# A four-layer residual block on one core: a constant matrix multiplied into unused banks by TensorE while it waits, and a deviation taken by logarithm and exponential

## The reference, cut to what matters

```python
x = x + L0(gn(x))   # 1x1 conv, norm, silu; a gate of 6 gaussian bases per group; 1x1 conv, norm, silu
x = x + L1(gn(x))   # the block below
x = x + L2(gn(x))   # 8-head attention over 256 tokens
x = x + L3(gn(x))   # deformable 3x3 convolution (offsets and mask from a 3x3 convolution)
```

```python
mu = jnp.mean(y, axis=-1, keepdims=True)
var = jnp.mean(jnp.square(y - mu), axis=-1, keepdims=True)
y = (y - mu) * jax.lax.rsqrt(var + 1e-05) * ln_g + ln_b
out = jnp.einsum('bld,od->blo', y, W_out)
```

## Time and profile before

| | us |
|---|---|
| median of 3 runs | 549.79 |
| lowest, highest | 548.02, 550.30 |
| the profiled execution: its time | 542.76 |
| the profiled execution: its span | 541.0 |
| mean granted share of TensorE's clock in it | 0.881 |

### The profile page before, as it was taken

The page is one execution under the profiler, slowest core; times in us unless marked ns, Lnnn a source line. Parts: engine busy times, 40 slices in busy tenths (PEclk is TensorE's granted clock), DMA queues, the critical chain, the costliest instruction groups (busy, mean ns, idle before and its releaser), DMA issues. The chain is left out here.

```text
span 541.0 us, 9049 instructions
## 1 busy us (share of the span) xinstructions
PE 408.6 (76%) x3218; PEld 207.1 (38%) x3218; DVE 355.1 (66%) x670; ACT 289.2 (53%) x509; POOL 119.2 (22%) x138
## 2 busy tenths in 40 slices
PE   1325681499999736488999999938269999999995
PEld 1114561245555413323333333325125544455442
DVE  4547786313365696988999998150446878788784
ACT  1459974113223413417888888812737668486441
POOL 4500003100000001864431111010004618156000
PEclk9856986599999985958999999977759999999998
DMA  5300000720000000882210000008674290742302
GB/s 138 116 0 1 0 0 0 146 48 1 0 1 0 1 0 1 233 274 81 80 41 3 4 2 2 2 22 180 155 158 105 52 213 2 175 89 63 70 2 78
DMA packets 21496, 34.35 MB, mean 64 GB/s; under 512 B 5376, under 2 KB 16336, under 8 KB 20688
## 3 DMA queue, kind: packets, MB, share of 16 engines
q1 hardware_dynamic: 17488, 24.94, 19.5%
q10 hardware_dynamic: 2688, 4.16, 3.2%
q0 software_dynamic: 1280, 4.72, 3.0%
HBM read 16.80 MB, written 4.64 MB: 40 GB/s over the span
## 5 line engine op out<-in xcount | busy, mean ns | idle before, releaser
L1259 DVE TENSOR_TENSOR L_s<-L_row_ps,L_cols 128x1024 f32<-128x1024 f32 x72 | 87.7, 1219 | 8.3 <-PE L_row_ps L1390 6.7
L877 DVE TENSOR_REDUCE L_mx<-L_ring 128x2 f32<-128x512 f32 x128 | 83.3, 687 | 10.4 <-PE L_ring L1000 9.9
L932 ACT ACTIVATE L_e<-L_ring 128x512 f32<-128x512 f32 x128 | 73.6, 597 | 20.9 <-PE L_ring L1013 18.9
L1411 PE MATMUL L_acc<-L_s,L_t_sb 128*64 128x256 f32 x576 | 79.8, 399 | 1.1 <-DVE L_s L1259 1.0
L1320 ACT ACTIVATE L_cols<-L_col_ps 128x512 f32<-128x512 f32 x72 | 42.8, 596 | 44.7 <-PE L_col_ps L1398 44.2
L1000 PE MATMUL L_ring<-stacks_k_st,stacks_q_st 64*128 64x256 bf16 x256 | 50.7, 300 | 7.0 <-DVE L_v_all L866 5.5
L1411 PEld LDWEIGHTS L_acc<-L_s,L_t_sb 128*64 128x64 f32 x576 | 35.5, 138 | 35.1 <-DVE L_s L1259 21.2
L1013 PE MATMUL L_ring<-stacks_q_st,stacks_k_st 64*128 64x256 bf16 x256 | 47.0, 281 | 1.7 <-DMA stacks_q_st<-L_m_parts 1.7
L1390 PE MATMUL L_row_ps<-L_hats,L_sel 48*128 48x512 bf16 x144 | 44.5, 391 | 0.0
L1033 PE MATMUL L_ctx_ps<-L_e,L_v_x 128*32 128x256 f32 x512 | 40.7, 391 | 0.0
L1381 PE MATMUL L_acc<-all_w_all,L_xn 64*128 64x192 f32 x96 | 26.3, 356 | 13.9 <-DVE L_t_sb L1239 13.9
(11 more groups left out here) (254 smaller groups left out, 765.4 us busy)
## 6 DMA issues: line engine op xcount, KB each, us to landing
L_hats<-L_parts SPq DMA_DIRECT2D x32, 216.0 KB, 5.0
L_hat<-L_offsets SPq DMA_DIRECT2D x24, 192.0 KB, 4.5
L_mask<-L_offsets SPq DMA_DIRECT2D x12, 192.0 KB, 4.6
stacks_q_st<-L_q_parts SPq DMA_DIRECT2D x12, 128.0 KB, 3.7
stacks_k_st<-L_k_parts ACTq DMA_DIRECT2D x12, 128.0 KB, 5.1
stacks_q_st<-L_q_parts POOLq DMA_DIRECT2D x12, 128.0 KB, 2.7
stacks_k_st<-L_k_parts POOLq DMA_DIRECT2D x12, 128.0 KB, 3.0
L_stack<-L_xpad SPq DMA_DIRECT2D x8, 162.0 KB, 5.7
```

The lines of the kernel that those rows point to most:

```text
L877: dve.tensor_reduce(mx[:, n % 2, :, head], ring[:, place(step) % 3].rearrange("p (q s) -> p q s", q=2), AX.X, ALU.max).then_inc(max_read, 1)
L932: act.activation(e[:, k], ring[:, 3 + v % 3], ACT.Exp, scale=HD2 ** -0.5).then_inc(e_ready, 1)
L1259: dve.tensor_tensor(s[:, q], row_ps[:, q], cols[:, t % 3:t % 3 + 1].broadcast_to([P, 2, 2 * N]), ALU.mult).then_inc(s_ready, 1)
L1411: mm = pe.matmul(acc[C * e:C * e + C, b, 0:N], t_sb[:, b, h, (KK * e + t) * C:(KK * e + t + 1) * C], s[:, q, h, e * N:(e + 1) * N], start= ...
```

## The change

1. **`keep_clock`**, new: `count` matmuls of `avg2` with itself (128x128, float32) into columns 0 to 127 of a PSUM bank that nothing reads at that time. It waits for nothing and signals nothing. It stands on PE at these places, 237 matmuls in all, in order: layer 0: 12 before the first norm and 5 after it, 4 after w_pre's matmuls, 22 after the second norm, 3 after the pooled vector's first matmul, 26 after the third norm (the block's last work on PE). Layer 1: 17 after the norm and ahead of the wait for `g_ready`, 4 ahead of the quads' first, in the last quad 5, 3 and 9 where the other quads have pieces of the next convolution, 14 at the end. Layer 2: 6 after the norm, 5 between the halves of v, 18 ahead of the wait for `v_all_ready`, and 1 in each of the 19 steps with v < 0. Layer 3: 25 after the norm and ahead of the first wait for `stack`, 40 between `weigh(0, 0, ...)` and `weigh(0, 1, ...)`.
2. **Layer 1's deviation**: in place of ACT's root, DVE's reciprocal and DVE's product stand a load of the table set that has logarithm and exponential, ACT's `Ln` of var into a new buffer `lnvar`, ACT's `Exp` with scale -0.5 (this gives 1/sqrt(var)), and DVE's product. In the last quad only `Exp` waits for `added`, not the read of `var`.
3. The layers' own step semaphores become one that the group norms already have. It moves and adds no instruction.

The diff, cut to its core:

```diff
+def keep_clock(pe, avg2, out, count):
+
+
+
+    for _ in range(count):
+        pe.matmul(out[:, 0:P], avg2[:], avg2[:], start=True, stop=True)
+
...
             def _(pe):
                 pe.wait_ge(avg_in, 16)
+                keep_clock(pe, avg2, y1[:, 6], 12)
                 gn_x.tensor(pe)
+                keep_clock(pe, avg2, y1[:, 6], 5)
                 weights.wait(pe, 0)
                 for h in range(NP // 2):
                     pe.wait_ge(xn_ready, 2 * h + 2)
                     pe.matmul(y1[:, 2 * h:2 * h + 2, :], w_pre[:], xn[:, 2 * h:2 * h + 2, :], start=True, stop=True).then_inc(y1_ready, 1)
+                keep_clock(pe, avg2, y2[:, 6], 4)
                 gn_1.tensor(pe)
+                keep_clock(pe, avg2, y2[:, 6], 22)
                 pe.wait_ge(z_ready, NP)
                 pe.matmul(s1, w_s1[:], pooled[:], start=True, stop=True).then_inc(s1_ready, 1)
+                keep_clock(pe, avg2, y2[:, 6], 3)
                 pe.wait_ge(h1_ready, 1)
                 pe.matmul(s2, w_s2[0:32, :], h1[:], start=True, stop=True).then_inc(s2_ready, 1)
                 pe.wait_ge(h2_w_ready, 1)
@@ -369,6 +383,7 @@
                             mm = pe.matmul(y2[:, ds(k, 1), :], w_post[:], t[:, q, j:j + 1, :], start=False, stop=(j == NB - 1))
                         mm.then_inc(t_used, 1)
                 gn_2.tensor(pe)
+                keep_clock(pe, avg2, y1[:, 6], 26)
 
-        o, var, sd = m.sb("o", [P, 2, N]), m.sb("var", [P, 2, N]), m.sb("sd", [P, 2, N])
+        o, var, lnvar, sd = (m.sb(n, [P, 2, N]) for n in ("o", "var", "lnvar", "sd"))
...
                 def over_deviation(q):
 
                     dve.wait_ge(sd_ready, q + 1)
-                    dve.reciprocal(sd[:], sd[:]).then_inc(scaled, 1)
-                    dve.wait_ge(scaled, 2 * q + 1)
                     dve.tensor_tensor(sd[:], o[:], sd[:], ALU.mult).then_inc(scaled, 1)
-                    dve.wait_ge(scaled, 2 * q + 2)
+                    dve.wait_ge(scaled, q + 1)
...
-                def deviation(q):
+                def deviation(q, last=False):
+
+
+                    act.preload_act_table_set("natural_log_exp_and_others")
                     act.wait_ge(o_copied, 2 * q + 4)
-                    act.activation(sd[:], var[:], ACT.Sqrt).then_inc(sd_ready, 1)
+                    act.activation(lnvar[:], var[:], ACT.Ln).then_inc(ln_ready, 1)
+                    act.wait_ge(ln_ready, q + 1)
+                    if last:
+                        act.wait_ge(added, NQ - 1)
+                    act.activation(sd[:], lnvar[:], ACT.Exp, scale=-0.5).then_inc(sd_ready, 1)
...
                 quad(0, True)
                 with act.Fori(1, NQ) as q:
                     quad(q, False)
-                act.wait_ge(added, NQ - 1)
-                deviation(NQ - 1)
+                deviation(NQ - 1, last=True)
 
             @block.tensor
             def _(pe):
                 gn.tensor(pe)
                 weights.wait(pe, 1)
+                keep_clock(pe, avg2, xs_ps[:, 0], 17)
                 pe.wait_ge(g_ready, 1)
...
                         conv_xs(q + 1, 0, 2)
+                    else:
+                        keep_clock(pe, avg2, xs_ps[:, 0], 5)
...
+                keep_clock(pe, avg2, xs_ps[:, 0], 4)
                 for g in range(NQ):
...
+                keep_clock(pe, avg2, xs_ps[:, 0], 14)
...
                 weights.wait(pe, 2)
+                keep_clock(pe, avg2, ring[:, 5], 6)
...
                     pe.matmul(k_bank(g), w_k[:], xn[:, 2 * g:2 * g + 2, :], start=True, stop=True).then_inc(k_ps_ready, 1)
                 for h in range(2):
+                    if h:
...
+                keep_clock(pe, avg2, ring[:, 4], 18)
                 pe.wait_ge(v_all_ready, 2)
...
                     if v + LAG < 8 * B:
                         largest(v + LAG)
+                    if v < 0:
+                        keep_clock(pe, avg2, ring[:, 4], 1)
...
                 weights.wait(pe, 3)
+                keep_clock(pe, avg2, row_ps[:, 1, 1], 25)
                 for g in range(NQ):
                     pe.wait_ge(stack_in[g], 64)
...
                 for k in range(6):
+                    if k == 1:
+                        keep_clock(pe, avg2, acc[:, 1], 40)
                     weigh(0, k, k, k)
```

More of the change, by code:

```diff
@@ L227, in layer0 @@
         avg_in, *x_in = m.sems("avg_in x_in0 x_in1")
-        (own, xn_ready, y1_ready, norm1_ready, z_ready, s1_ready, h1_ready, s2_ready, h2_ready, h2_w_ready,
+        (xn_ready, y1_ready, norm1_ready, z_ready, s1_ready, h1_ready, s2_ready, h2_ready, h2_w_ready,
          par_ready, exp_in, exp_out, coef_ready) = m.sems(
-            "own xn_ready y1_ready norm1_ready z_ready s1_ready h1_ready s2_ready h2_ready h2_w_ready "
+            "xn_ready y1_ready norm1_ready z_ready s1_ready h1_ready s2_ready h2_ready h2_w_ready "
             "par_ready exp_in exp_out coef_ready")
@@ L279, in _ @@
                 dve.sem_inc(norm1_ready, 1)
-                step = Steps(dve, own)
+                step = Steps(dve, signals.own, signals.own_steps)
                 dve.wait_ge(h2_ready, 1)
@@ L316, in _ @@
                 step(dve.tensor_tensor(zc0[:], zc0[:], c0[:], ALU.add))
+                signals.own_steps = step.n
                 with dve.Fori(0, NP // 2) as i:
@@ L476, in layer1 @@
             "conv_ready acts_ready bt_ready xt_ready bt_copied v_ready kv_ps kv_ready y_ps y_own y_ready cen_y sq_ready o_ready var_ready o_copied")
-        added, scaled, sd_ready = m.sems("added scaled sd_ready")
+        added, scaled, sd_ready, ln_ready = m.sems("added scaled sd_ready ln_ready")
         with nc.Block() as block:
@@ L677, in quad @@
                         conv_xs(q + 1, 2, 4)
+                    else:
+                        keep_clock(pe, avg2, xs_ps[:, 0], 3)
                     pe.wait_ge(kv_ready, q + 1)
@@ L683, in quad @@
                         conv_xs(q + 1, 4, 8)
+                    else:
+                        keep_clock(pe, avg2, xs_ps[:, 0], 9)
                     pe.wait_ge(y_ready, 2 * q + 4)
@@ L763, in layer2 @@
         scratch = [nc.dram_tensor(f"L2_{n}_parts", (NQ, 3, 2, HD2, 4, 2, 2 * N), BF16, kind="Internal").ap() for n in "qk"]
[L765 to L766 removed]
+        (xn_ready, q_ps_ready, k_ps_ready, full_ready, hi_ready, mid_ready, parts_ready, v_ps_ready, v_all_ready,
+         pool_own) = m.sems("xn_ready q_ps_ready k_ps_ready full_ready hi_ready mid_ready parts_ready v_ps_ready v_all_ready pool_own")
         stored = m.sems(" ".join(f"stored_{s}{g}" for g in range(NQ) for s in "qk"))
```

7 lines of the change are left out of this document (3 added, 4 removed).

## The result

| | before | changed |
|---|---|---|
| median of 20 runs, us | 548.15 | 551.16 |
| lowest, highest, us | 543.16, 552.69 | 546.99, 556.96 |
| ratio to before, 95% interval | | 1.0069 [1.0039, 1.0100] |
| the profiled execution: span, us | 541.0 | 550.6 |
| mean granted clock in it | 0.881 | 0.911 |

The account below looks back on a forecast made before the run. The prediction saw a low PE clock in the layers' openings and layer 1's reciprocals on the path; terms summed to 11.75, rounded to 12, off the median 549.79 gave 537.8 us, range 532.5 to 545.0.

Parts of the forecast that it names:

- layer 2's part: Layer 2's opening and lead-in: 1.4 us saved in all, with the singles fitting PE's spare time while DVE sets the steps.
- The price: Every added matmul: 0.23 us from the moment the clock is full, 0.43 before.
- rival A: Layer 2's opening and layer 3's weighings: the clock falls again in gaps, gain only 8.5, time 541.3 us; chance 0.28.
- rival C: All blocks: added matmuls do not lift the clock and stay at 0.43 to 0.48; 10 slower, 560 us; chance 0.05.
- Deviation, 3.65: Layer 1's tail: without reciprocals, with logarithm and exponential, 3.65 us saved, or 2.85 if the table load drains.
- Layer 1's opening, 2.2: Layer 1's norm and first quad run faster at the full clock: 2.2 us saved after 0.2 for the barrier.
- The barrier: Before layer 1: the 26 take 8 us and end level with the barrier, at worst 0.35 late.
- Layer 0, 1.8: Layer 0's opening and middle: norm, w_pre's matmuls and those after ACT's silu come sooner, 1.8 us saved.
- Layer 2's opening, 1.4: Layer 2's norm and first matmuls run faster: 1.4 us saved if the clock lasts from 199 to 205.
- Offsets, 1.3: Layer 3's first stretch: the 25 make the first four convolutions take 2.79 instead of 4.28; 1.3 us saved.
- The 40, 1.4: Layer 3's second stretch: weighings and samples come sooner, 1.4 us saved with the clock full, 0 without.
- the signs named for the clock row: Slices 3, 7, 15 to 16 and 27 to 31 rise if right; 16 to 18 and 29 to 30 stay at 5 in rival A.

Follow-up runs that it names:

- e3: The kernel before with only the 19 singles of layer 2's lead-in added, root and reciprocal kept: 557.99 us, ratio to before 1.0166.
- e9: The changed kernel with all 19 singles and 26 instead of 18 matmuls ahead of layer 2's lead-in: 543.69 us, ratio to before 0.9891.
- e2: The changed kernel with every count of keep_clock set to 0, so the new deviation alone: 544.11 us, ratio to before 0.9900.
- e1: The changed kernel without the 19 single matmuls of layer 2's lead-in: 540.31 us, ratio to before 0.9841.
- e4: The changed kernel with layer 1's deviation by root and reciprocal again, all 237 added matmuls kept: 559.64 us, ratio to before 1.0189.
- e8: The changed kernel with a single only in every other step of layer 2's lead-in, 9 instead of 19: 538.89 us, ratio to before 0.9857.
- e10: The changed kernel with the new deviation and the added matmuls of layers 0 and 1 alone: 538.54 us, ratio to before 0.9791.
- e12: The changed kernel without singles, the 40, layer 3's 25 or layer 2's opening 6, and 19 for the barrier's 26: 538.92 us, ratio to before 0.9813.
- e5: The changed kernel without the 19 singles and without layer 3's 40: 541.38 us, ratio to before 0.9916.
- e7: The changed kernel without the singles and with 52 instead of 40 between layer 3's first and second weighing: 540.88 us, ratio to before 0.9900.

## Why the prediction was wrong, step by step

**The step that failed** is in layer 2's part: "the 19 singles add 4.4 us to PE in the lead-in, where it has 4 us to spare in 18 ... DVE sets those steps." It put the singles at nothing; they measured 8.8 us (the changed kernel's lead-in) and 9.9 (e3), and PE set the steps. Three things were wrong with it.

- *The price.* 0.23 us was read from a dense run of equal weight loads, and dense blocks ran at it (26 in 5.97 us, e9). In turn with a score pair, a single holds PE up to the next pair for 0.42 us at the full clock (224.43 to 224.85, e9) and for 0.73 at the low one (229.18 to 229.91, changed kernel). To a step of 0.60 it adds 0.14 and 0.66. Why it costs more there than in a block is not shown; that its weight load is less well hidden would be a reason.
- *The spare time.* The 4 us of a whole window are no use to steps in which PE is nearly full: at the low clock a pair takes PE 0.53 us up to the single behind it (228.65 to 229.18), and DVE's pace leaves 0.60 to 0.62, so less than 0.1 us was free for 0.73. The spare time sat in the waits for ACT and the transfer. Sum and capacity belong to one step.
- *The clock.* I took it as full from 199 us on, and rival A let it fall but priced only the lost gain. That the added work itself would then run at the low price, on a path where it mattered, was priced in rival C alone, for blocks only.

With the singles at 9.9 us (e3) and the other terms as forecast, the sum would have been 2 us faster; the medians differ by 3 us the other way. With the terms as measured below, 3.65 for the deviation, 1.8 for layer 1 and 0.9 for layer 0, less 9.9, the sum is 3.5 us slower, which is near it.

The other terms: **Deviation, 3.65**: right, 3.66 in the profile, 3.7 in e2, and layer 1's quads kept their 17.3 us. The table load took 1.28 us and the logarithm, waiting for `var` anyway, began 0.61 us behind it. The Trainium skill (ScalarE: Activation LUTs, What ACT_TABLE_LOAD costs) counts a drain with each change of sets, some 2.7 us in all; with it behind the load the logarithm could not have begun before 196.1. It began at 195.31, so this trace does not show that drain. **Layer 1's opening, 2.2**: right in kind and nearly in size, 1.8 to 1.9 by stages. **The barrier**: 0 to 0.35 late was forecast, 0.9 in the profile after, 0 in e1's. The sum gave the 26 8 us and they took 8.87; an added matmul at the low clock took 0.48 us (six in 2.91, layer 2's opening), where the sum had 0.43. **Layer 0, 1.8**: not settled. In the changed kernel's profile the 12 ended 2.2 us before the norm's matmul, which ran at the low clock as ever (0.59), w_pre's matmuls took 5.04 us for 5.14, and L374 still took 1.03. In twelve profiles with these blocks the layer ended between 90.9 and 94.4 us, 92.6 on the mean, in three without added matmuls at 93.4 to 93.5: perhaps half of the term. In four of the twelve (e4, e8, e10, e12) the gate's matmul, L374 here, ran at the full clock and began at 28.6 to 28.7 us, where it began at 30.3 to 30.5 in the three without; in e5 and e9 it ran at the full clock and came late all the same. With the same blocks in all twelve, that is luck and not design. **Layer 2's opening, 1.4**: wrong. The 14 ended at 197.9, the norm's second matmul took 0.60 and the first q 1.91; the clock had fallen, as rival A said, and the first score waited for a transfer. The opening got 1.5 us longer in this profile; with the same blocks it took 25.1 to 27.9 us in six profiles, with none in layers 1 and 2 25.3 to 25.8 in four, so the blocks brought nothing there, and whether they cost something stays open. **Offsets, 1.3**: 1.5 came, and the waits behind them took back all but some 0.6, if that (e12). **The 40, 1.4**: nothing, as rival A said.

So rival A's mechanism was right in both its places and its size was wrong, since it stopped at what is lost. Rival C's sign was right and its reason wrong: the matmuls do lift the clock. Of the signs named for the clock row some slices were miscounted in the earlier trace rows: layer 1's opening is slices 7 and 8, and slices 17 and 31 stood at 9 already.

## What to carry to other kernels

Work that is added to keep an engine's clock up has to reach the work it is meant for: blocks that ended two or three microseconds early bought nothing, and what came after them ran at the low clock all the same. Inside a loop, price an added instruction at the slow clock and in its place in the step, and compare step by step with the engine that sets the pace; half as many were free here where all of them cost 9 to 10 us. Read a gain at marks in the timeline, stage by stage, where a transfer can make a whole run 5 us longer by itself.

## What the runs showed of the hardware

- A single short gap of PE can be followed by the low clock: it stayed full after 0.44 us (e9) and 1.09 us (before, layer 3), and was low soon after 1.93 (e7), 2.07 and 3.10 us (changed kernel). The gap's length alone does not decide: in layer 0's loop of the changed kernel PE idled for 2.59 us and the six matmuls behind it (12 records) took 2.86 us, as the ones before them.
- A step of one 64x256 bf16 score pair and one 128x128 float32 matmul, 0.74 us, held the full clock for 15 us (e9); once the clock was low, the same step at 1.26 us, with PE hardly idle, did not raise it for over 20 us (changed kernel, 228 to 249). In this trace a PE that was busy throughout did not get the clock back by that alone; the block of 26 ahead of layer 1 (8.87 us) and layer 2's first dense matmuls (1.91 us a pair of passes, then 1.02) did.
